# An attention layer with LayerNorm: four staging places for values, spread loads of x, other projection lists per gap, and loads issued by SyncE

## The chip, the core and the metric

The kernel runs on one core of a Trainium2 chip. The metric is the time of one execution on the device in microseconds (us).

## What is computed

One transformer layer for 16 images of 30 x 30 tokens of 512 features, 8 heads of 64, all in float32, with a bias on the scores that depends on the distance of two tokens on the grid:

```python
q, k, v = proj(wq, bq), proj(wk, bk), proj(wv, bv)     # x_seq @ w + b, split in 8 heads
scores = einsum('bhqd,bhkd->bhqk', q, k) / sqrt(d_k)
scores = scores + spatial_bias_matrix[None, None]      # by |dh| + |dw|
attn = softmax(scores, axis=-1)
ctx = einsum('bhqk,bhkd->bhqd', attn, v)
out = ctx @ wo + bo
resid = out + x_seq
out = (resid - mu) * rsqrt(var + 1e-5) * ln_gamma + ln_beta
```

## The kernel before

The images run one after the other through one software pipeline. Heads go in 4 pairs p. A pair's 30 rows of queries make 15 units, so an image has 60 units u, numbered 0 to 59. For one unit TensorE makes the scores of two heads against all 900 tokens (L684, 16 matmuls into one of two halves of s_ps), VectorE adds the bias and takes the least value (L966; q is negated), ScalarE takes the exponential and its sum (L803). The keys lie in two halves on different partitions, so their two maxima and sums are exchanged: SyncE issues four small DMAs own to other for two units together (L486, `exchange`), GpSimd finds the difference (L1099, L1102, `leads`), ScalarE its exponential (L811, `ratios`), GpSimd the weight (L1108 to L1113, `totals`), ScalarE scales the probabilities (L819, `normalise`), VectorE transposes them (L982, `turn`), and TensorE multiplies a group of up to five units by the values (L702, `context`), which ScalarE copies to ctx_sb (L831).

Every engine has a program of its own, written out in a fixed order by a function `body(im, u)`, called for u = 0 to 59 of each image. The engines stand in the same numbering but not at the same time, since they wait for each other by semaphores. In body u TensorE issues (u even only) the scores of units u+6 and u+7, then the contexts that `PV_UNITS` puts there, then the items that `GAPS[u]` lists; two bodies, u and u+1, are called a step here, by the even number. ScalarE does in body u: evictions that `EVICT` puts there, a context to keep, the exponentials of unit u+6, in odd bodies the ratios of u+3, the normalising of u+2, then issues of loads. VectorE: scores of u+6, the transpose of u, a turn of x, sums and norms of output tiles. GpSimd: totals or leads, 1/std, splits of x, bias, splits of the context. SyncE: stores of values, in odd bodies the exchange for u+5 (it waits for the exponentials of u+6), then stores, residual loads, loads of x.

The items of a gap are the projections, which share two banks of r_ps in turn in the order of `SEQUENCE`:
- ("piece", p, j), L603: half of k or half of q of pair p; pieces 4 and 5 belong to pairs 0 and 1 of the next image. ScalarE evicts it (L760, `keep_piece`). After the second half it issues the load of the next pair's weights, 512 KB (L741).
- ("value", t), L619: a tile of 120 or 90 tokens of v of the next image. ScalarE puts it into stage (L777, `stage_value`), which has two places, t % 2, and waits at L775 until the store of the tile two before has landed. SyncE stores it to v_dram (L478), from where ScalarE issues the loads of a pair's values by `LOADS`, four for a pair (L793).
- ("out", t), L645: an output tile of the image before. GpSimd splits the context into two float32r parts first (L1124, L1126, body by `SPLIT_UNITS`) and adds the bias to the residual (L1155), VectorE sums and normalises (L996 to L1010).

An item is evicted one body after its gap, a second item that is not an output tile two bodies after it. Float32 products are made of three float32r products, so an item has 12 matmuls.

x of the next image comes in 8 tiles of up to 128 tokens, four DMAs each (L496, `load_x`), into four places; VectorE turns it (L954, body `X_UNITS[t]` - 1) into x_turned, which lies in the last part of ctx_sb, and GpSimd splits it into xt (L1137, L1144, body `X_UNITS[t]`). Tiles 0 to 3 are loaded at `LOAD_X`, tiles 4 to 7 at `X_UNITS[t - 4]`, each as four issues in a row. Image 0 has no output tiles, the last one (image 15) no values and no pieces 4 and 5, and ends with its own output tiles ("final").

## Time and profile before

| | |
|---|---|
| median of 3 runs | 3177.74 us (3175.3 to 3180.98) |
| profiled execution, whole | 3174.42 us |
| its span | 3172.5 us |
| TensorE clock granted, mean | 0.991 of full |
| busy | TensorE 3027.3, VectorE 2649.1, ScalarE 2709.9, GpSimd 1615.2 us |
| DMA | 266.8 MB, mean 84 GB/s |

The span goes from the first instruction to the last end; the execution's own time has a little around it. Busy time is the sum of an engine's instructions; a wait lies in none of them, and "waiter <- releaser" in a row says which engine's result ended it. Matmuls overlap, and their ends are modelled. The windows view gives, for a stretch of time in us from the span's start, its length and then for TensorE's matmuls, its weight loads, VectorE, ScalarE and GpSimd the busy us and the instructions, then the granted clock (1.00 is full), the share of DMA engines busy and GB/s. "SPq" and "ACTq" are the queues in which SyncE and ScalarE issue DMAs; the us of such a line are the issuing, not the transfer.

### The profile page before, as it was taken

The numbers are of one execution on the slowest core, as the hardware profiler recorded it, in microseconds if no ns is written. First come the engines' busy times: TensorE is split into PE (matmuls) and PEld (weight loads), VectorE is DVE, ScalarE is ACT, GpSimd is POOL, SyncE is SP. The second block draws the span as 40 slices with busy tenths as digits, with TensorE's granted clock in tenths as the row PEclk, the third lists the DMA queues.
The fourth block names the chain that finished last, engine by engine and source line by source line (L and its number), as shares of the span: only waits on it lengthen the run. The fifth ranks groups of instructions, "written<-read, shape, count | busy, mean of one in ns | idle before, by whom it ended". The sixth has DMA issues, their size and how long they took to land.

```text
span 3172.5 us, 111090 instructions
## 1 busy us (share of the span) xinstructions
PE 3027.3 (95%) x44584; PEld 2073.6 (65%) x44584; DVE 2649.1 (84%) x5594; ACT 2709.9 (85%) x6839; POOL 1615.2 (51%) x3277
## 2 busy tenths in 40 slices
PE   7999999999999999999999999999999999999986
PEld 5666666666666666666666666666666666666654
DVE  3878889798897978879798897988979788797887
ACT  4988898888989888898888988888898898988885
POOL 1346445464553745546464454645536455464643
PEclk9999999999999999999999999999999999999998
DMA  7332423324243342323324233241433423233221
GB/s 206 72 82 73 99 63 95 81 71 109 57 97 85 78 98 68 86 78 92 88 73 102 60 95 84 76 104 54 97 82 78 102 69 90 74 91 89 73 66 28
DMA packets 523228, 266.81 MB, mean 84 GB/s; under 512 B 329274, under 2 KB 460346, under 8 KB 522590
## 3 DMA queue, kind: packets, MB, share of 16 engines
q1 hardware_dynamic: 375479, 127.82, 18.3%
q10 hardware_dynamic: 147232, 131.88, 14.1%
q8 instruction: 351, 5.75, 0.8%
q14 instruction: 166, 1.36, 0.1%
HBM read 194.10 MB, written 63.44 MB: 81 GB/s over the span
## 4 chain that ended last, share of the span: by engine, by line
PE 47%; DVE 15%; ACT 14%; SPq 11%; DMA 6%; issue 5%; POOL 2%; ACTq 0%; DVEq 0%
PE r_ps L603 13%; PE pv_ps L702 13%; PE s_ps L684 12%; ACT prob L803 7%; PE r_ps L645 6%; ACT prob L819 5%; SPq L496 5%; SPq L486 5%; DVE prob L966 5%; DVE prob_t L982 5%; DMA other<-own 4%; PE r_ps L619 3%; DVE stats L998 2%; DVE tokens L996 1%; DMA v_dram<-stage 1%
## 5 line engine op out<-in xcount | busy, mean ns | idle before, releaser
L803 ACT ACTIVATE prob<-prob,own 128x450 f32<-128x450 f32 x1920 | 1265.3, 662 | 142.3 <-DVE own L966 127.1
L966 DVE CUSTOM_DVE_ANT_0 prob<-s_ps,window 128x450 f32<-128x450 f32 x1920 | 1121.9, 621 | 286.1 <-PE s_ps L684 206.4
L982 DVE STREAM_TRANSPOSE prob_t<-prob 128x960 f32<-128x960 f32 x960 | 1126.6, 1174 | 140.1 <-ACT prob L819 139.8
L819 ACT ACTIVATE prob<-prob,weight 128x450 f32<-128x450 f32 x1920 | 1173.2, 660 | 52.8 <-POOL weight L1113 51.1
L684 PE MATMUL s_ps<-k_sb,q_sb 64*32 64x450 f32 x15360 | 856.4, 548 | 42.9 <-DVE own L966 39.9
L702 PEld LDWEIGHTS pv_ps<-prob_t,values 64*64 64x64 f32 x23040 | 730.0, 133 | 152.8 <-issue 80.1
L702 PE MATMUL pv_ps<-prob_t,values 64*64 64x150 f32 x23040 | 783.6, 290 | 8.5 <-DVE prob_t L982 8.4
L603 PE MATMUL r_ps<-xt,w_sb 128*128 128x450 f32 x3072 | 686.1, 373 | 27.5 <-ACT k_sb L760 13.5
L603 PEld LDWEIGHTS r_ps<-xt,w_sb 128*128 128x128 f32 x3072 | 572.1, 190 | 172.8 <-issue 69.8
L1099 POOL TENSOR_TENSOR lead<-own,other 128x4 f32<-128x4 f32 x480 | 96.6, 201 | 925.9 <-DMA other<-own 924.4
L1113 POOL TENSOR_TENSOR weight<-total,minus_one 128x4 f32<-128x4 f32 x480 | 501.0, 1044 | 37.6
L684 PEld LDWEIGHTS s_ps<-k_sb,q_sb 64*32 64x32 f32 x15360 | 229.0, 106 | 419.2 <-issue 296.1
L645 PE MATMUL r_ps<-wo_sb,ctx_split 128*120 128x512 f32 x1536 | 391.5, 405 | 32.1 <-DVE ctx_split L1017 10.9
L619 PE MATMUL r_ps<-wv_sb,xt 128*120 128x512 f32 (+1 forms) x1536 | 380.7, 400 | 18.2 <-POOL xt L1144 18.1
L645 PEld LDWEIGHTS r_ps<-wo_sb,ctx_split 128*120 128x120 f32 x1536 | 273.4, 184 | 175.5 <-issue 84.4
L619 PEld LDWEIGHTS r_ps<-wv_sb,xt 128*120 128x120 f32 (+1 forms) x1536 | 262.2, 176 | 158.9 <-issue 64.8
L803 ACT ACTIVATION_READ_ACCUMULATOR prob<-prob,own 128x1 f32 x1920 | 364.0, 190 | 0.0
L1108 POOL TENSOR_TENSOR total<-ratio,other 128x4 f32<-128x4 f32 x480 | 111.8, 233 | 424.7 <-ACT ratio L811 406.9
L811 ACT ACTIVATE ratio<-lead 128x4 f32<-128x4 f32 x480 | 94.1, 196 | 95.5 <-POOL lead L1102 94.0
L1155 POOL TENSOR_TENSOR tokens<-tokens,bo_all 120x512 f32<-120x512 f32 x120 | 160.6, 1344 | 0.0
L966 DVE DVE_READ_ACCUMULATOR2_ANT own<- 128x1 f32 x1920 | 157.6, 82 | 0.0
L1126 POOL TENSOR_TENSOR ctx_split<-ctx_sb,ctx_split 128x480 fp32r<-128x480 f32 x120 | 145.0, 1209 | 9.8
(63 smaller groups left out, 1475.9 us busy)
## 6 DMA issues: line engine op xcount, KB each, us to landing
w_sb<-w_split ACTq DMA_DIRECT2D x126, 512.0 KB, 3.9
values<-v_dram ACTq DMA_DIRECT2D x256, 240.0 KB, 3.3
other<-own SPq DMA_DIRECT2D x1920, 1.0 KB
tokens<-in_x SPq DMA_DIRECT2D x420, 64.0 KB, 2.6
tokens<-in_x SPq DMA_DIRECT2D x109, 240.0 KB, 3.6
out<-tokens SPq DMA_DIRECT2D x105, 240.0 KB, 2.8
v_dram<-stage SPq DMA_DIRECT2D x90, 240.0 KB, 3.0
v_dram<-stage SPq DMA_DIRECT2D x30, 180.0 KB, 2.3
```

The lines of the kernel that those rows point to most:

```text
L486: sp.dma_start(other[QUAD * a:QUAD * a + QUAD, s, :, :], own[QUAD * c:QUAD * c + QUAD, s, :, :]).then_inc(exchanged[s], 16)
L603: last = pe.matmul(r_ps[:, bank, 0:HALF], w_sb[:, kind, a, k, :], xt[:, c, k, columns(half)], start=(k == 0 and i == 0), stop=(k == KT - 1 ...
L619: last = pe.matmul(r_ps[0:n, bank, :], xt[:, a, k, at:at + n], wv_sb[:, c, k, :], start=(k == 0 and i == 0), stop=(k == KT - 1 and i == PA ...
L645: last = pe.matmul(r_ps[0:TT, bank, :], ctx_split[:, t % 2, a, k, :], wo_sb[:, c, k, :], start=(k == 0 and i == 0), stop=(k == PAIRS - 1 a ...
L684: last = pe.matmul(s_ps[row:row + QUAD, u % 2, head, 0:HALF], q_sb[d, p % 2, q0:q0 + QUAD], k_sb[d, p % 2, columns(r)], start=True, stop=T ...
L702: last = pe.matmul(pv_ps[d, a, 0:n * GRID].rearrange("d (u w) -> d u w", u=n), values[half, p % 2, j, d], prob_t[half, g % 2, 0:n, head, Q ...
L803: nc.scalar.activation(prob[:, im.unit(u) % RING, head, 0:HALF], prob[:, im.unit(u) % RING, head, 0:HALF], ACT.Exp, scale=-1.0, bias=own[: ...
L819: nc.scalar.activation(prob[:, im.unit(u) % RING, head, 0:HALF], prob[:, im.unit(u) % RING, head, 0:HALF], ACT.Copy, scale=weight[:, s, c: ...
L966: nc.vector.tensor_tensor_reduce(prob[:, im.unit(u) % RING, head, 0:HALF], s_ps[:, u % 2, head, 0:HALF], window[:, w0:w0 + HALF // GRID, : ...
L982: nc.vector.transpose(out=prob_t[:, g % 2, v % PER_GROUP, :, :].rearrange("p h k -> p (h k)"), in_=prob[:, im.unit(u) % RING, :, :].rearra ...
L1113: nc.gpsimd.tensor_tensor(weight[:, s, :], total[:, s, :], minus_one[:, :], ALU.pow).then_inc(weight_done, 1)
L1155: nc.gpsimd.tensor_tensor(y, y, bo_all[0:rows(t), :], ALU.add).then_inc(res_bias, 1)
```

## The change

- Values go through four staging places, `STAGE_SLOT`, the third and fourth in the part of ctx_sb where x_turned lay. x_turned now lies where ctx_split does. The waits are changed to fit.
- `LOAD_X` has eight entries; a tile's four DMAs are issued two in that body, two in the next. `X_UNITS` is later from tile 3 on.
- `GAPS` has another list of items for each gap, with `SPLIT_UNITS` to fit. Output tiles come in pairs at 14 and 22, pieces in pairs at 18, 24, 28, 48 and 54, values in pairs at 32, 38 and 42.
- The loads of weights and values inside the images are issued by SyncE, behind the exchange of the same body, and not by ScalarE. A residual is loaded six bodies after an output tile's eviction and not five.

```diff
-SPLIT_UNITS = [0, 0, 3, 5, 6, 10, 13, 15]
-LOAD_X = [20, 22, 26, 29]
-X_UNITS = [30, 31, 32, 33, 34, 36, 38, 40]
+SPLIT_UNITS = [0, 0, 3, 5, 9, 13, 15, 16]
+LOAD_X = [24, 26, 29, 31, 33, 35, 37, 39]
+X_UNITS = [30, 31, 32, 36, 37, 40, 41, 43]
+STAGE_SLOT = [0, 1, 2, 3, 0, 1, 0, 1]
+STAGES = 4
...
-GAPS = {2: pieces(1, (3,)) + [out(0)], 4: [out(1), out(2)], 8: [out(3)] + pieces(2, (0,)), 12: [out(4)] + pieces(2, (1,)),
-        14: [out(5)] + pieces(2, (2,)), 18: [out(6)] + pieces(2, (3,)), 22: [out(7)] + pieces(3, (0,)),
-        24: pieces(3, (1, 2)), 28: pieces(3, (3,)), 32: [value(0), value(1)], 34: [value(2), value(3)],
-        38: [value(4), value(5)], 42: [value(6)] + pieces(4, (0,)), 44: pieces(4, (1, 2)), 48: pieces(4, (3,)),
-        52: [value(7)] + pieces(5, (0,)), 54: pieces(5, (1,)), 58: pieces(5, (2,))}
+GAPS = {2: [out(0)] + pieces(1, (3,)), 4: [out(1)], 8: [out(2)] + pieces(2, (0,)), 12: [out(3)] + pieces(2, (2,)),
+        14: [out(4), out(5)], 18: pieces(2, (3, 1)), 22: [out(6), out(7)], 24: pieces(3, (0, 2)), 28: pieces(3, (3, 1)),
+        32: [value(0), value(1)], 34: [value(2)], 38: [value(3), value(4)], 42: [value(5), value(6)], 44: pieces(4, (2,)),
+        48: pieces(4, (0, 1)), 52: pieces(4, (3,)) + [value(7)], 54: pieces(5, (0, 1)), 58: pieces(5, (2,))}
...
             def load_values(im, p, n):
...
+                if n == 0:
+                    if p == 0:
+                        for i in range(STAGES):
+                            sp.wait_ge(v_kept[i], kept_in(i, b + 1))
+                    if pair > 1:
+                        sp.wait_ge(pv_full, PAIR_GROUPS * (pair - 1))
...
+                for work in im.evicted(u):
+                    if work[0] == "piece" and PIECES[work[2]][1] and not (im.last and work[1] == PAIRS - 1):
+                        next_weights(im, *work[1:])
...
+                if u in LOADS and not (im.last and LOADS[u][0] == PAIRS):
+                    load_values(im, *LOADS[u])
                 for work in im.out_tiles(u - 4) + im.finals(u - 2):
                     store(im, work)
-                for work in im.out_tiles(u - 5):
+                for work in im.out_tiles(u - 6):
...
+                    for t in range(X_TILES):
+                        if u == LOAD_X[t] and t >= SLOTS:
+                            sp.wait_ge(x_turn, X_TILES * im.b + t - SLOTS + 1)
...
+                        for a in range(128 // QUAD):
+                            if u == LOAD_X[t] + a // 2:
+                                load_x(im.b + 1, t, a)
...
-                    act.wait_ge(v_kept[t % 2], 16 * (NT // 2 * (im.b + 1) + t // 2))
+                    i = STAGE_SLOT[t]
+                    if i >= 2 and im.first:
+                        act.wait_ge(wq_kept, 16 * 2 * PAIRS)
+                    elif i >= 2:
+                        act.wait_ge(split_lo, NT * im.b)
+                    act.wait_ge(v_kept[i], kept_in(i, im.b + 1) + 16 * STAGE_SLOT[:t].count(i))
...
                 if g == GROUPS - PAIR_GROUPS - 1 and not im.last:
-                    act.wait_ge(x_lo, X_TILES * (im.b + 1))
+                    for i in range(2, STAGES):
+                        act.wait_ge(v_kept[i], kept_in(i, im.b + 2))
...
-                elif t == 0:
-                    dve.wait_ge(split_lo, NT * im.b)
+                if t == 0 and not im.first:
+                    use = ("out", NT - 1)
+                    dve.wait_ge(bank_full[bank_of(use)], im.use(use) + 1)
```

## Rows read from the trace of the kernel before

**Rows 1.** The page: busy time by engine, shares of the chain by engine.

```profile
PE 3027.3 (95%) x44584; PEld 2073.6 (65%) x44584; DVE 2649.1 (84%) x5594; ACT 2709.9 (85%) x6839; POOL 1615.2 (51%) x3277
...
PE 47%; DVE 15%; ACT 14%; SPq 11%; DMA 6%; issue 5%; POOL 2%; ACTq 0%; DVEq 0%
```

**Rows 2.** Windows view, images 1 to 14: busy us by engine (instructions), clock, DMA, GB/s.

```profile
254.47:2955.66 2701.19, 2621.35 (x38977) 1797.94 (x38976) 2302.51 (x4876) 2358.08 (x5972) 1434.30 (x2889) 1.00 0.33 83
```

**Rows 3.** Windows view, image 7: steps 4, 8, 34, 44; then 10, 14, 24, 28, 38.

```profile
1426.31:1435.01 8.70, 7.73 (x57) 4.69 (x56) 8.28 (x17) 7.12 (x18) 8.05 (x15) 1.00 0.21 63
1440.67:1448.81 8.14, 7.32 (x60) 4.75 (x56) 7.85 (x18) 7.26 (x21) 5.68 (x10) 1.00 0.21 54
1524.59:1532.64 8.05, 7.64 (x58) 4.39 (x57) 5.86 (x12) 5.55 (x14) 5.13 (x9) 1.00 0.45 71
1559.13:1567.60 8.47, 7.11 (x58) 4.84 (x57) 5.14 (x11) 8.17 (x20) 2.29 (x7) 1.00 0.27 74
1448.81:1454.47 5.66, 5.66 (x154) 4.27 (x153) 5.41 (x11) 4.32 (x13) 4.24 (x7) 1.00 0.50 140
1461.93:1469.03 7.10, 7.10 (x57) 4.84 (x56) 6.85 (x16) 5.14 (x13) 6.61 (x13) 1.00 0.39 111
1494.72:1501.48 6.76, 6.76 (x57) 4.92 (x56) 6.55 (x14) 6.10 (x16) 2.54 (x8) 1.00 0.64 141
1507.14:1511.48 4.34, 4.34 (x48) 2.66 (x44) 3.23 (x9) 4.20 (x13) 1.43 (x4) 1.00 0.31 73
1538.29:1545.73 7.44, 7.44 (x60) 4.76 (x56) 3.87 (x8) 4.91 (x14) 2.13 (x4) 1.00 0.58 169
```

**Rows 4.** Waits of TensorE in images 1 to 14: us, times, longest.

```profile
PE s_ps L684 <- DVE own L966: 20.5, 25, 1.5
PE r_ps L619 <- POOL xt L1144: 15.1, 13, 2.1
PE r_ps L645 <- POOL ctx_split L1126: 9.7, 14, 1.0
PE r_ps L645 <- ACT q_sb L760: 9.3, 12, 1.7
PE pv_ps L702 <- DVE prob_t L982: 8.4, 17, 0.8
PE r_ps L603 <- ACT k_sb L760: 7.6, 13, 0.8
PE r_ps L603 <- ACT stage L777: 6.9, 14, 0.5
```

**Rows 5.** Waits of ScalarE in images 1 to 14.

```profile
ACT prob L803 <- DVE own L966: 108.4, 101, 3.5
ACT ratio L811 <- POOL lead L1102: 76.4, 81, 3.1
ACT stage L777 <- DMA v_dram<-stage: 65.7, 28, 3.5
ACT prob L819 <- POOL weight L1113: 46.8, 57, 2.1
```

**Rows 6.** Timeline of SyncE's queue, image 7: start, us, engine, line, operation, count.

```profile
1517.20 6.10 SPq L496 DMA_DIRECT2D tokens<-in_x  x8
1523.34 2.53 SPq L486 DMA_DIRECT2D other<-own  x4
```

**Rows 7.** Timeline of GpSimd after the exchange issued at 1523.34.

```profile
1527.10 0.20 POOL L1099 TENSOR_TENSOR lead<-own,other 128x4 f32<-128x4 f32 x1 [2.75 <-DMA other<-own]
```

**Rows 8.** Timelines of SyncE, ScalarE, GpSimd, image 7: an exchange beside a weight load.

```profile
1461.95 3.64 SPq L486 DMA_DIRECT2D other<-own  x4
...
1462.28 0.34 ACTq L741 DMA_DIRECT2D w_sb<-w_split  x1
...
1467.88 0.20 POOL L1099 TENSOR_TENSOR lead<-own,other 128x4 f32<-128x4 f32 x1
```

**Rows 9.** The page: a weight load, KB, median us from issue to landing.

```profile
w_sb<-w_split ACTq DMA_DIRECT2D x126, 512.0 KB, 3.9
```

More of the change, by code:

```diff
@@ L171, in groups @@
         before = [] if self.first else [(Before(self), g) for g in pv_groups(u + UNITS)]
-        return before + [(self, g) for g in pv_groups(u, self.last) if u < UNITS or self.last]
+        return before + [(self, g) for g in pv_groups(u) if u < UNITS or self.last]
     def background(self, u):
@@ L279, in attention_layernorm @@
         ctx_sb = sb("ctx_sb", [128, PAIRS, S])
+        with nc.sbuf_tensor("x_turned", [128, 2, D], F32) as x_turned:
+            pass
         ctx_split = sb("ctx_split", [128, 2, 2, PAIRS, TT], F32R)
@@ L383, in attention_layernorm @@
         v_staged = sem("v_staged")
-        v_kept = [sem(f"v_kept{i}") for i in range(2)]
+        v_kept = [sem(f"v_kept{i}") for i in range(STAGES)]
         v_in = [sem(f"v_in{i}") for i in range(2)]
@@ L418, in staged, with kept_in @@
             n = value_rows(t)[2]
-            return turned_flat[0:n, t * D:t * D + D] if im is pro else stage[0:n, t % 2, :]
+            return turned_flat[0:n, t * D:t * D + D] if im is pro else (
+                stage[0:n, STAGE_SLOT[t], :] if STAGE_SLOT[t] < 2 else stage_too[0:n, STAGE_SLOT[t] - 2, :])
+        def kept_in(i, images):
+            return 16 * STAGE_SLOT.count(i) * images
         def out_no(im, work):
@@ L477, in keep_value @@
                         sp.wait_ge(v_in[i], 64 * PAIRS // 2 * im.b)
-                sp.dma_start(v_dram[(im.b + 1) % 2, half, j:j + n, :], staged(im, t)).then_inc(v_kept[t % 2], 16)
+                sp.dma_start(v_dram[(im.b + 1) % 2, half, j:j + n, :], staged(im, t)).then_inc(v_kept[STAGE_SLOT[t]], 16)
             def exchange(im, x):
@@ L593, in piece @@
                     first_xt_ready(NT - 1)
-                if j == 0 and p == PAIRS and im is not pro:
-                    pe.wait_ge(x_lo, X_TILES * (im.b + 1))
+                if p == PAIRS and im is not pro:
+                    pe.wait_ge(x_lo, X_TILES * im.b + x_tiles_to(HALF * (half + 1)))
                 if half == 0:
@@ L672, in scores @@
                         if mine:
-                            pe.wait_ge(bank_free[bank], mine[-1])
+                            pe.wait_ge(bank_free[bank], max(mine))
                         elif p == 1:
@@ L761, in keep_piece @@
                                      bias=bias[:, p % PAIRS:p % PAIRS + 1]).then_inc(bank_free[bank], 1)
-                if half and not (im is pro and p == PAIRS) and not (im.last and p == PAIRS - 1):
+                if half and im is pro and p > PAIRS:
                     next_weights(kind, p)
@@ L779, in stage_value @@
                 act.nop(nofuse=True).then_inc(v_staged, 1)
-            def load_values(im, p, i):
-                b, p = (im.b, p) if p < PAIRS else (im.b + 1, 0)
-                pair = PAIRS * b + p
-                if i == 0:
-                    if p == 0:
-                        for bank in range(2):
-                            act.wait_ge(v_kept[bank], 16 * NT // 2 * (b + 1))
-                    if pair > 1:
-                        act.wait_ge(pv_full, PAIR_GROUPS * (pair - 1))
-                a, r = divmod(i, 2)
-                row = 2 * QUAD * a + QUAD * r
-                act.dma_start(values[row:row + QUAD, p % 2, :, :],
-                              v_dram[b % 2, r, :, 128 * p:128 * p + 128].rearrange("(j k) d -> k j d", k=QUAD)
-                              ).then_inc(v_in[p % 2], 16)
             def exponentials(im, u):
@@ L901, in body @@
                     return
-                if im.first and u == 0:
-                    use = ("bv_wo", 0)
-                    act.wait_ge(bank_full[bank_of(use)], pro.use(use) + 1)
-                    act.wait_ge(lo_done["wo"], 1)
-                    for i in range(4):
-                        load_values(im, 0, i)
-                if u in LOADS and not (im.last and LOADS[u][0] == PAIRS):
-                    load_values(im, *LOADS[u])
                 for t in range(NT):
@@ L977, in turn @@
                 if im.first and u == 0:
-                    for i in range(2):
-                        dve.wait_ge(v_kept[i], 16 * NT // 2)
+                    for i in range(STAGES):
+                        dve.wait_ge(v_kept[i], kept_in(i, 1))
                 if v % PER_GROUP == 0 and not known(group, 1):
@@ L1132, in x_split_hi @@
                 if t == 0:
-                    for use in pieces(PAIRS - 1, (2, 3)):
+                    for use in pieces(PAIRS - 1):
                         pool.wait_ge(bank_full[bank_of(use)], im.use(use) + 1)
@@ L1182, in body @@
                         x_split_lo(im, t)
-                for work in im.out_tiles(u + 2):
+                for work in (im.out_tiles(1) if u == 0 else []) + im.out_tiles(u + 2):
                     add_bias(im, work)
```

57 lines of the change are left out of this document (35 added, 22 removed).

## The prediction

> **What bounds the kernel now.** I read the page first. TensorE is busy 3027.3 us, 95% of the span, VectorE and ScalarE 84% and 85%, and the chain that ended last runs through TensorE for only 47% and touches every engine, SyncE's queue with 11% [rows 1]. So TensorE paces the kernel, and the others touch it at places; the question is which places, and what each costs. For that the windows view over images 1 to 14, which run the same program: 2701.19 us, 192.94 an image, TensorE busy 2621.35, 187.2 an image, clock 1.00 throughout [rows 2]. ScalarE is busy 2358.1 / 14 = 168.4 us an image and VectorE 164.5.
>
> Then single steps. A step is two units: TensorE issues two units of scores and after them a context group, or one or two of what a gap lists (piece, value or output tile). Without a stall a step takes 5.66 us with a context, 4.34 with one piece, 6.76 with two, 7.10 with a piece and an output tile, 7.44 with two value tiles; in all five TensorE's busy time is the whole window [rows 3]. An output or value tile alone makes 7.10 - (6.76 - 4.34) = 4.68. The old lists have 12 context steps, 8 mixed ones, 2 with two pieces, 4 with one piece and 4 with two tiles: 12 x 5.66 + 8 x 7.10 + 2 x 6.76 + 4 x 4.34 + 4 x 7.44 = 185.4 us. An image takes 192.9, so stalls cost 7.6 us an image. TensorE's named waits sum to 77.9 us in 14 images, 5.6 an image [rows 4]; the other 2.0 are matmuls stretched beside a wait. In image 7 step 4 is 8.70 instead of 7.44, step 8 8.14 instead of 7.10, step 34 8.05 instead of 7.44, step 44 8.47 instead of 6.76 [rows 3].
>
> **The change part by part.**
>
> *New list of projections.* Its work is the same, only grouped otherwise: 12 context steps, 5 with two tiles, 5 with two pieces, 4 mixed, 2 with one tile, 2 with one piece: 67.9 + 37.2 + 33.8 + 28.4 + 9.4 + 8.7 = 185.4 us. Nothing is gained on TensorE itself, all of it is in the stalls.
> - Step 4 held out(1) and out(2). Out(2)'s split is GpSimd's, in body 3, and came late 14 times of 14, 9.7 us; the first waited for ScalarE to empty its bank, 9.3 us [rows 4]. Now step 4 holds out(1) alone, and out(2) comes at step 8, four bodies later. Both waits go: 1.3 us by image 7.
> - Step 8's stall is the second set of scores waiting for VectorE (20.5 us at 25 places, most of them here). VectorE has two output tiles to sum and one to normalise around step 6 and is busy 7.85 of step 8's 8.14 us [rows 3]. The new list has such doubles at 14 and 22. Behind 22 stands a step of 6.76 instead of 5.66, so VectorE has 1.1 us more, which is what the stall costs here: nothing there. Behind 14 stands a context step as before, but out(3) is now first in its step and not second, so VectorE gets it a piece (2.4 us) earlier. Between 0 and the 1.04 us of step 8; I take 0.4, nearer to nothing, since the 2.4 us are more than the stall.
> - Step 44 had two pieces straight behind a value and a piece; each bank was emptied by ScalarE just too late (7.6 + 6.9 us), and ScalarE is busy 8.17 of 8.47 us there [rows 3, 4]: it was behind. Now 44 has one piece, 42 two values, 48 two pieces with a context step between. Gone, 1.7 us by image 7. New pairs in neighbouring steps are 12/14, 22/24, 52/54. In the first two the later pair's first item wants the bank of an item that VectorE empties, as at the old 12 and 14, where step 14 took its bare 7.10; at 52/54 a piece has only the value tile (2.8 us) behind it before the next image's first scores want it. If ScalarE is late by more there, step 54 stalls; old step 54 is preceded by a full step of slack. 0 to 1.1 us; I take 0, since ScalarE has longer steps (6.76, 7.10) to catch up in.
>
> *Four staging places.* ScalarE waited for the store of two tiles earlier 28 times, 65.7 us, 2.35 each [rows 5], and it is in order: exponentials, normalising and evictions queue behind it, and VectorE's transposes and TensorE's contexts (8.4 us, steps 40 and 0) behind these. With four places, and value tiles spread over 32 to 42, a place is filled again four bodies after it was filled or later, where it is two now; a body is 3.2 us and the wait 2.35, so one body more would do. The wait goes. TensorE gets back its own part, the context waits, 0.6 an image; in image 0, which has no output tiles, ScalarE paces, and there the 2 x 2.35 = 4.7 us count fully. Places 2 and 3 lie where the turned x lay; the waits put in for that (split_lo, v_kept before a context is kept) are for things done several bodies earlier. Cost 0.
>
> *Spread loads of x.* An exchange of row statistics costs SyncE 2.53 us for its four issues; eight loads of x in a row cost 6.10, so 0.76 each [rows 6]. Of the 32 of an image 20 stand in bodies 29 to 33, and exchanges queued behind: the wait of ScalarE's ratio for lead is 76.4 us in 81 places [rows 5]. The lateness went on to GpSimd's splits of x and from there to value tiles at 32 and 34, 15.1 us [rows 4]. Now each body from 24 to 40 has at most two loads: per step 2.53 + 4 x 0.76 = 5.6 us. The tightest stretch is steps 34 to 38, 4.68 + 5.66 + 7.44 = 17.8 us: there SyncE has 3 x 5.6 and seven single issues (value stores and loads, a residual), at 0.34 to 0.76 each 2.4 to 5.3, together 19 to 22. SyncE is late there by 1 to 4 us, against over 6 behind the eight loads of rows 6. Price: x of tile 2 arrives nearly when VectorE turns it (issued in body 30, turned in 31), up to 2 us of VectorE with nothing queued that TensorE needs before step 34; no cost. For value tiles whose x is split in the same step (31/32, 37/38, 41/42) between 0 and the 1.1 us an image they cost today; I take 0.3.
>
> *Loads issued by SyncE.* ScalarE's issue of 0.34 us ran beside its activations (0.34 us at 1462.28) [rows 8], so taking 24 away gives ScalarE 0 to 24 x 0.34 = 8.2 us; I take 0, because the queue's issue isn't in its busy time. SyncE gets the 8.2 us; it holds 30 x 2.53 = 76, x loads of 32 x 0.76 = 24 and some 24 other issues of 0.34 to 0.76, 8 to 18 (an estimate), so it goes from 56 to 61% of an image to 60 to 66%. What is queued behind an issue is the next exchange. In SyncE's order all of these loads stand behind an exchange, none just ahead of one. That helps: clean, lead starts 1.23 us after the exchange's last issue (1525.87 to 1527.10) [rows 6, 7]; with a weight load issued by ScalarE into its middle, it is 1465.59 to 1467.88, 2.3 us, and the four issues took 3.64 us instead of 2.53 [rows 8]. I count no gain of its own for that: it pays for the risk. SyncE's new waits (a piece's bank full, v_kept, pv_full) are all for events before the exchange that it has just waited for.
>
> The Trainium skill speaks against this part. "DMA: Bandwidth & Descriptors", section "Queues, rings and completion order", says that SP and ACT each have one ring on the same 16 engines, that a ring is consumed in order, and that an engine takes turns between rings. So a small exchange behind a weight load of its own ring would have to wait for all of it, where today it takes turns. [...] It is the second rival below.
>
> **The sum,** against the profiled execution (3172.5 us span, 3174.4 in all, 3.3 below the median of 3177.7). Stalls that stay: 0.4 + 0.3 + 0.2 (contexts at 0 and 40) = 0.9 of 7.6 us, so 6.7 us an image, 94 in 14. Image 15 has steps 4 and 8: 2.3. Image 0: 4.7. Together 101: 3073.4, on the median's scale 3077.
>
> **Rivals.**
> 1. *The stalls move.* The doubles at 14 and 22 each make a stall of step 8's size (1.04), the three second value tiles one of step 34's (0.61), the new neighbour at 54 one of 1.1: 2.1 + 1.8 + 1.1 = 5.0 against 7.6, a gain of 2.6 x 14 + 7 = 43: 3134. For it: the pattern exists today; against it: each has more slack than its old twin. Half of it is as likely as all: 3105 to 3134.
> 2. *The exchange becomes the bound (slower).* If the loads keep the next exchange's packets waiting, each of 16 value loads by 1.1 us and each of 8 weight loads by 2.2 (2.3 - 1.2 seen once, doubled for the whole ring), ScalarE waits 35 us more for ratio an image. Its own total today is 168.4 + (76.4 + 46.8) / 14 = 177.2, so it would need 212 with nothing hidden, and with half hidden 195; against 192.9 that is +2 x 14, 3205. It decides from 0.65 us for each of the 24 loads, since ScalarE has 15.7 us to spare. Against it: between the end of one exchange and the next start there are about 3.9 us (a mean step of 6.4 less 2.5), and a weight load lands in 3.9 [rows 9].
> 3. *It does not do what it says:* SyncE, blocked on the exchange, issues loads so late that they are waited for, or the four places only shift ScalarE's wait to VectorE (108.4 us of ScalarE's waits are for VectorE already [rows 5]). Then within some us of today: 3178.
>
> **How the numbers follow.** Forecast 3077 with its own range 3060 (no stall stays) to 3100 (2.5 us an image stay): 0.65. Rival 1: 0.21. Rival 3: 0.04. Rival 2: 0.10. Range 3058 to 3134, which leaves out rivals 2 and 3 and the ends of the others. Faster by over 0.2% (about what a measurement of this kernel can tell from no change): 0.86; within: 0.03; slower: 0.11.
>
> **What would show it.** After the change: an image of 186 to 187.5 us with TensorE's waits under 1.5; no wait of stage for v_dram; ratio's wait for lead at most half; the waits of L645 for ctx_split and for q_sb gone, as that of pieces for k_sb; scores waiting for VectorE at step 18 under 0.4 us. Wrong: ratio waits of over 2 us behind SyncE's loads, VectorE's double at 14 showing over 1 us at step 18, or second value tiles waiting for x. The prediction fails high if step lengths without stall grow over 5.66, 6.76 and 7.44.

## The result, and the profile after

| | before | after |
|---|---|---|
| median | 3179.4 us (3175.3 to 3185.0, 4 runs) | 3256.2 us (3245.6 to 3259.9, 4 runs) |
| ratio, 95% interval | | 1.0239 (1.022 to 1.0259) |
| profiled execution, span | 3172.5 us | 3258.1 us |
| an image, mean of 14 | 192.94 us | 199.12 us |
| granted TensorE clock, mean | 0.991 | 0.978 |

The change costs 77 us, where 101 were to be gained. The two spans differ by 85.6 us: 14 x 6.18 = 86.5 in images 1 to 14, 2.4 more ahead of image 0, 2.4 less in it and 0.9 less in the last image and the end.

First the page of after: busy time, shares of the chain, groups of instructions, DMA issues (count, KB, median us from issue to landing).

```profile
PE 3060.8 (94%) x44584; PEld 2085.6 (64%) x44584; DVE 2643.7 (81%) x5594; ACT 2707.4 (83%) x6839; POOL 1599.1 (49%) x3277
...
PE 41%; SPq 14%; ACT 13%; DVE 12%; DMA 8%; issue 6%; POOL 6%; DVEq 0%; ACTq 0%; POOLq 0%
...
w_sb<-w_split SPq DMA_DIRECT2D x123, 512.0 KB, 4.7
...
tokens<-in_x SPq DMA_DIRECT2D x420, 64.0 KB, 3.2
```

TensorE has the same 44584 matmuls and is busy 33.5 us longer [rows 1]; SyncE's queue and DMA have grown in the chain, from 11 and 6% to 14 and 8%. A weight load lands 4.7 us after its issue instead of 3.9 [rows 9].

The windows view of after: images 1 to 14; then steps 4, 8, 18, 32 and 34 of image 7, a part of step 34, and steps 42 and 44.

```profile
254.47:3042.16 2787.69, 2656.68 (x38977) 1812.38 (x38976) 2296.81 (x4873) 2354.51 (x5966) 1418.92 (x2884) 0.98 0.32 81
1462.46:1467.13 4.67, 4.67 (x46) 2.59 (x45) 4.43 (x13) 4.64 (x13) 4.02 (x6) 1.00 0.02 1
1473.69:1482.52 8.83, 7.31 (x57) 4.75 (x57) 8.54 (x18) 8.83 (x26) 5.13 (x12) 1.00 0.16 44
1508.63:1516.41 7.78, 7.03 (x60) 4.79 (x57) 7.49 (x18) 7.26 (x20) 3.52 (x8) 1.00 0.15 36
1554.38:1566.04 11.66, 7.74 (x60) 4.63 (x57) 4.71 (x12) 4.77 (x13) 5.44 (x10) 1.00 0.62 133
1566.04:1574.81 8.77, 7.35 (x44) 3.74 (x45) 8.34 (x17) 8.11 (x21) 3.15 (x8) 0.61 0.22 45
1567.06:1573.88 6.82, 5.43 (x25) 3.09 (x26) 6.39 (x16) 6.58 (x17) 1.84 (x6) 0.50 0.15 38
1593.52:1605.03 11.51, 9.24 (x60) 5.74 (x56) 7.56 (x17) 8.10 (x21) 4.71 (x13) 0.85 0.38 106
1605.03:1609.35 4.32, 4.32 (x46) 2.67 (x46) 3.08 (x8) 3.74 (x9) 1.38 (x3) 1.00 0.32 82
```

Steps 4 and 44 are bare, as forecast. Step 8 takes 8.83 us where 8.14 were and 7.10 expected; step 18, behind the pair of output tiles, 7.78 for a bare 6.76. The large losses are at 32 (11.66 for 7.44), 34 (8.77 for 4.68) and 42 (11.51 for 7.44). In step 32 VectorE and ScalarE are busy less than half of the time: they wait too.

The waits of after in images 1 to 14, first of TensorE, then of the others (us in total, times, longest).

```profile
PE s_ps L727 <- DVE own L990: 120.3, 89, 3.4
PE r_ps L688 <- POOL ctx_split L1150: 6.8, 11, 1.2
PE r_ps L662 <- POOL xt L1168: 3.2, 6, 0.8
...
DVE x_turned L978 <- DMA tokens<-in_x: 184.9, 65, 7.3
...
ACT prob L835 <- DVE own L990: 189.4, 112, 7.2
ACT prob L851 <- POOL weight L1137: 139.4, 79, 6.2
ACT ratio L843 <- POOL lead L1126: 35.2, 51, 1.7
...
POOL tokens L1179 <- DMA tokens<-in_x: 78.4, 28, 5.3
```

TensorE waits for little but VectorE's treatment of scores, six times as long as before (20.5 us [rows 4]), and VectorE's own long wait is for x: 184.9 us at its turn, L978. An image has 13.2 us of it: 2.6 at the turn of tile 1, 6.4 at tile 2, 2.8 at tile 6, 1.4 at the others. The stall can be followed in image 7. SyncE's queue and VectorE (start, us, engine, line, operation, in brackets the idle time before it and who ended it):

```profile
1555.47 0.59 SPq L503 DMA_DIRECT2D w_sb<-w_split  x1
1556.10 1.61 SPq L528 DMA_DIRECT2D tokens<-in_x  x2
1557.77 0.61 SPq L503 DMA_DIRECT2D w_sb<-w_split  x1
1558.43 1.26 SPq L528 DMA_DIRECT2D tokens<-in_x  x2
...
1555.48 0.71 DVE L978 STREAM_TRANSPOSE x_turned<-tokens 128x512 f32<-128x512 f32 x1 [3.40 <-DMA tokens<-in_x]
1557.18 1.17 DVE L1006 STREAM_TRANSPOSE prob_t<-prob 128x960 f32<-128x960 f32 x1
1564.20 0.71 DVE L978 STREAM_TRANSPOSE x_turned<-tokens 128x512 f32<-128x512 f32 x1 [5.85 <-DMA tokens<-in_x]
```

and TensorE beside them:

```profile
1557.32 0.99 PE L727 MATMUL s_ps<-k_sb,q_sb 64*32 64x450 f32 x16 [1.96 <-DVE own L990]
1558.24 5.84 PE L662 MATMUL r_ps<-wv_sb,xt 128*120 128x512 f32 x24
1566.04 0.99 PE L727 MATMUL s_ps<-k_sb,q_sb 64*32 64x450 f32 x16 [1.96 <-DVE own L990]
1568.45 1.75 PE L727 MATMUL s_ps<-k_sb,q_sb 64*32 64x450 f32 x16 [1.42 <-DVE own L990]
1570.14 4.74 PE L662 MATMUL r_ps<-wv_sb,xt 128*120 128x512 f32 x12
```

The four loads of x's tile 2 go in two pairs, each right behind a 512 KB weight load. The last is issued by 1559.69 and the tile is there at 1564.20, 4.5 us later. VectorE has been ready since 1558.35. Behind the turn stand, in VectorE's order, the biased scores of units 38 and 39, and TensorE can't write units 40 and 41 over them before: it has two value tiles to do, finishes them at 1564.08 and stands still to 1566.04 and again before 1568.45. The last of TensorE's lines shows what follows: a value tile of 12 matmuls at 4.74 us, where a pair of them took 5.84 just before.

The first stall in step 32, 1.96 us before 1557.32, has another source: the turn of tile 1 at 1555.48, which waited 3.40 us. No weight load is near that tile, whose second half is issued at 1551.13; it is issued late and turned soon. On the mean of 14 images TensorE stands still 1.2 us before the scores of unit 39, behind tile 1, and 2.4 and 1.2 us before those of 40 and 41, behind tile 2.

Over the 14 images I set the start of each even unit's scores against the bare step lengths of [rows 3]. That gives the loss per image by groups of steps, for this kernel and all others but x_early, residual_early and tail_residual_6:

| us per image, steps | 0, 2 | 4 | 6, 8 | 12-18 | 20-30 | 32, 34 | 36-42 | 44 | sum |
|---|---|---|---|---|---|---|---|---|---|
| before | 0.6 | 1.6 | 1.3 | 0.5 | 0 | 1.4 | 0.7 | 1.4 | 7.6 |
| after | 0 | 0 | 2.3 | 1.4 | 0 | 7.6 | 2.5 | 0 | 13.8 |
| loads_scalar | 0 | 0 | 2.3 | 2.3 | 0 | 0.9 | 2.6 | 0 | 8.1 |
| before_loads_sync | 0 | 1.6 | 1.5 | 0.7 | 0 | 1.7 | 0.6 | 1.4 | 7.6 |
| before_staging | 0.6 | 1.9 | 1.2 | 0.5 | 0 | 1.3 | 0.1 | 1.0 | 6.6 |
| weights_scalar | 0 | 0 | 2.2 | 1.5 | 0.1 | 2.5 | 2.9 | 0 | 9.2 |
| loads_last | 0 | 0 | 2.2 | 1.8 | 0 | 3.0 | 3.9 | 0 | 10.8 |
| turn_later | 0 | 0 | 2.3 | 1.5 | 0 | 4.7 | 2.0 | 0 | 10.5 |
| two_weights_later | 0 | 0 | 2.1 | 1.5 | 0.1 | 1.7 | 8.5 | 0 | 13.8 |
| two_weights_at_31 | 0 | 0 | 2.1 | 1.5 | 0 | 1.6 | 4.0 | 0 | 9.2 |
| lists_mended | 0 | 0 | 2.5 | 1.9 | 0.1 | 0 | 1.2 | 0 | 5.7 |
| mended_unpaired | 0 | 0 | 2.4 | 0.2 | 3.1 | 0.1 | 1.7 | 0 | 7.5 |
| staging_spread | 0.1 | 1.5 | 1.5 | 0.6 | 0 | 2.8 | 0.2 | 0 | 6.8 |
| staging_tail | 0 | 1.4 | 1.7 | 0.4 | 0 | 1.2 | 0 | 0 | 4.8 |

(Steps 46 to 58 are within 0.1 everywhere.) From before to after 0.6 + 1.6 + 1.4 = 3.6 us an image are gained at 0 to 4 and at 44, and 6.2 + 1.8 + 1.0 + 0.9 = 9.9 lost at 32 and 34, 36 to 42, 6 and 8, and 12 to 18: 6.3, against 6.2 by the period.

### The profile page after: what moved, and what is told of

Read it like the earlier page. It is cut to its first block, busy times and chain, and to the rows that moved or that the text cites. A ratio compares the mean times of both kernels' runs of the same rounds, so it can differ in the third digit from the quotient of the medians.

```text
span 3258.1 us, 111151 instructions
## 1 busy us (share of the span) xinstructions
PE 3060.8 (94%) x44584; PEld 2085.6 (64%) x44584; DVE 2643.7 (81%) x5594; ACT 2707.4 (83%) x6839; POOL 1599.1 (49%) x3277
## 4 chain that ended last, share of the span: by engine, by line
PE 41%; SPq 14%; ACT 13%; DVE 12%; DMA 8%; issue 6%; POOL 6%; DVEq 0%; ACTq 0%; POOLq 0%
PE r_ps L646 11%; PE s_ps L727 11%; PE pv_ps L745 10%; SPq L494 7%; ACT prob L835 7%; DMA tokens<-in_x 6%; PE r_ps L662 6%; ACT prob L851 5%; DVE prob L990 5%; DVE prob_t L1006 4%; SPq L528 4%; PE r_ps L688 3%; DMA other<-own 2%; POOL tokens L1179 1%; POOL weight L1137 1%
## 5 line engine op out<-in xcount | busy, mean ns | idle before, releaser
L727 PE MATMUL s_ps<-k_sb,q_sb 64*32 64x450 f32 x15360 | 876.6, 555 | 150.6 <-DVE own L990 149.4
L646 PE MATMUL r_ps<-xt,w_sb 128*128 128x450 f32 x3072 | 674.3, 373 | 5.7 <-ACT prob_t L825 3.7
L662 PE MATMUL r_ps<-wv_sb,xt 128*120 128x512 f32 (+1 forms) x1536 | 401.5, 417 | 3.5 <-POOL xt L1168 3.5
L662 PEld LDWEIGHTS r_ps<-wv_sb,xt 128*120 128x120 f32 (+1 forms) x1536 | 280.3, 187 | 150.4 <-issue 65.5
L978 DVE STREAM_TRANSPOSE x_turned<-tokens 128x512 f32<-128x512 f32 x120 | 77.6, 647 | 199.2 <-DMA tokens<-in_x 198.8
```

The source lines that it names most:

```text
L646: last = pe.matmul(r_ps[:, bank, 0:HALF], w_sb[:, kind, a, k, :], xt[:, c, k, columns(half)], start=(k == 0 and i == 0), stop=(k == KT - 1 ...
L662: last = pe.matmul(r_ps[0:n, bank, :], xt[:, a, k, at:at + n], wv_sb[:, c, k, :], start=(k == 0 and i == 0), stop=(k == KT - 1 and i == PA ...
L727: last = pe.matmul(s_ps[row:row + QUAD, u % 2, head, 0:HALF], q_sb[d, p % 2, q0:q0 + QUAD], k_sb[d, p % 2, columns(r)], start=True, stop=T ...
```

## The experiments

Ratios are to the kernel before on the same chip, with 95% intervals. In the cuts of code below `...` stands for what is left out, also inside a line, and what stands behind `#` is my note.

| | median us | ratio |
|---|---|---|
| loads_scalar | 3183.4 | 1.0015 (1.000 to 1.003) |
| before_loads_sync | 3175.4 | 0.9993 (0.9981 to 1.0005) |
| x_early | 3231.2 | 1.0168 (1.0149 to 1.0186) |
| before_staging | 3155.2 | 0.9932 (0.9918 to 0.9947) |
| two_weights_later | 3268.0 | 1.0288 (1.0268 to 1.0307) |
| residual_early | 3248.8 | 1.0224 (1.0198 to 1.0249) |
| lists_mended | 3146.3 | 0.9897 (0.9874 to 0.992) |
| staging_tail | 3134.2 | 0.9864 (0.9847 to 0.988) |
| weights_scalar | 3198.1 | 1.0055 (1.0031 to 1.0079) |
| loads_last | 3219.9 | 1.0132 (1.010 to 1.0164) |
| turn_later | 3213.3 | 1.0101 (1.0078 to 1.0124) |
| staging_spread | 3161.0 | 0.9935 (0.9911 to 0.9959) |
| two_weights_at_31 | 3200.0 | 1.007 (1.0053 to 1.0087) |
| mended_unpaired | 3173.6 | 0.9984 (0.9975 to 0.9994) |
| tail_residual_6 | 3136.5 | 0.9869 (0.9854 to 0.9884) |

**Which part costs it.** Two small parts of the change, one value load issued in body 56 and not 55 and pieces 4 and 5 waiting for no more of x than they read, are in every kernel made from after, and no run takes them apart. loads_scalar is after with the weight and value loads issued by ScalarE again:

```diff
-                for work in im.evicted(u):
-                    if work[0] == "piece" and ...:
-                        next_weights(im, *work[1:])          # sp
...
+                if half and not (im is pro and p == PAIRS) and not (im.last and p == PAIRS - 1):
+                    next_weights(kind, p)                    # act; load_values too
```

> The changed kernel, but weights and values are loaded by ScalarE again, in the bodies in which they were. Theory A (x is loaded too few bodies before VectorE turns it; VectorE waits for it 184.9 us in 14 images of the changed kernel and TensorE's scores behind it): the loads of x keep their places, so most of the wait stays, 100 us or more, and the time is 3200 to 3250. Theory B (weights, values, x and exchanges in one queue of SyncE: two weight loads are issued just ahead of the second half of x tile 2): VectorE's wait for x falls under 50 us and the time to 3180 or below.

3183.4 us: 73 of the 77 us are gone (1.0239 to 1.0015), so theory A is not the whole of it. VectorE's wait for x fell from 184.9 to 94.8 us, not under 50. before_loads_sync does the opposite, that part alone on the kernel before (SyncE's `next_weights` and `load_values` as in the change):

> The kernel before, with only the issue of weights and values moved to SyncE. Theory B: most of the loss is here, 3230 to 3260. Theory A: x tiles 0 to 3 are loaded early as before, so within 15 us of the kernel before, 3165 to 3195.

3175.4, no difference that can be measured, so theory B alone isn't it either. The loads on SyncE cost nothing by themselves, and the rest of the change costs 5.7 us by itself (3183.4 - 3177.7); the 73 us are of the two together. In before_loads_sync x is issued as early as ever. In before tile 2 of x had been issued 9.9 us ahead of step 32's start on the mean of 14 images, VectorE was ready to turn it at 1.3 and waited 0.2. In after the last issue is at 4.9, 15 us later, VectorE is ready at 3.2 and waits 6.4. loads_scalar has the same lists and late issues: last issue at 1.1, a wait of 1.3.

**Is it the lateness of x?** x_early issues the first tiles earlier, all else as after:

```diff
-LOAD_X = [24, 26, 29, 31, 33, 35, 37, 39]
+LOAD_X = [20, 22, 28, 30, 33, 35, 37, 39]
```

> The changed kernel with LOAD_X = [20, 22, 28, 30, 33, 35, 37, 39] instead of [24, 26, 29, 31, ...]: x tiles 0 to 3 one to four bodies earlier, all loads still by SyncE. Theory A: VectorE's wait for x in step 32 (116 us of 185) goes down by 80 or more, steps 32 and 34 lose 5 of their 7.7 us of excess, and the time is 3150 to 3190. Theory B: the queue only moves its lateness, the time stays over 3220.

3231.2: a third of the loss gone. Theory A had 3150 to 3190, theory B over 3220. It isn't the clean test I meant. SyncE stood still for the place of tiles 2 and 3, since output tiles 6 and 7 are now made at 22 and stored only in body 27 (waits of SyncE in x_early):

```profile
SPq L494 <- ACT prob L835: 925.8, 385, 7.6
SPq L528 <- DMA out<-tokens: 67.2, 28, 4.1
```

So tile 2's last issue came at 4.3 and not ahead of the turn. The new list of projections holds x back too; LOAD_X alone can't undo it. turn_later moves the other end, the turn of tile 2, one body back:

```diff
-X_UNITS = [30, 31, 32, 36, 37, 40, 41, 43]
+X_UNITS = [30, 31, 33, 36, 37, 40, 41, 43]
```

> The changed kernel with x tile 2 turned and split one body later (X_UNITS[2] = 33 instead of 32), loads where they were. If VectorE's in-order wait for tile 2 is what stops the scores in steps 32 and 34 (7.7 us an image), one body (3.2 us) more takes off 3 us an image of VectorE's wait and 30 to 60 us of the time: 3195 to 3225. If the value tile of step 34 then waits for the split instead, nothing is won: 3240 to 3260.

3213.3: the wait falls from 6.4 to 4.1 us and the loss at 32 and 34 from 7.6 to 4.7 an image. What stands behind the waiting turn counts, and how long it waits.

**Number or place of the loads.** weights_scalar gives only the eight weight loads of an image back to ScalarE, the 16 value loads stay:

```diff
-                if half and im is pro and p > PAIRS:
+                if half and not (im is pro and p == PAIRS) and not (im.last and p == PAIRS - 1):
                     next_weights(kind, p)
```

> The changed kernel with only the weight loads (8 an image, 512 KB) issued by ScalarE again; values stay with SyncE. The measured 73 us between all loads by SyncE (3256) and by ScalarE (3183) come from weight loads ahead of x tile 2 and of the last residual in SyncE's one ring: then this recovers 50 or more of the 73, under 3205. If it is the number of issues on SyncE (16 value loads are 2 of 3), it recovers about a third, 3225 to 3240.

3198.1: 58 of the 77 us gone. Tile 2 waits 1.0 us, its data there 1.9 us after the last issue, not 4.6. That looks as if a queue of their own kept the weights out of x's way, but the trace shows another reason. ScalarE issues the two weight loads of bodies 29 and 30 earlier than SyncE did, 7.9 and 3.0 us ahead of step 32's start on the mean, where SyncE issued them 0.9 and 3.0 us behind it. They now fall beside tile 1, and although they stand in the other queue that tile lands late: 4.7 us after its last issue on the mean, in after 2.7, with the same value load and stores of output ahead of it in SyncE's queue. Image 5 of weights_scalar, queues of SyncE and ScalarE, then VectorE:

```profile
1128.15 2.39 SPq L528 DMA_DIRECT2D tokens<-in_x  x2
1126.23 0.33 ACTq L781 DMA_DIRECT2D w_sb<-w_split  x1
1128.69 0.33 ACTq L781 DMA_DIRECT2D w_sb<-w_split  x1
1136.68 0.71 DVE L975 STREAM_TRANSPOSE x_turned<-tokens 128x512 f32<-128x512 f32 x1 [4.80 <-DMA tokens<-in_x]
```

The last part of tile 1 is issued by 1130.54 and there only 6.1 us later. It took 5.4 to 6.8 us in the five images in which the second weight load was issued less than 2 us ahead of that point, 2.7 to 4.7 in the other nine. The 2.5 us an image that are still lost at step 32 are tile 1's. loads_last leaves all on SyncE, but puts them behind everything else of a body:

```diff
+                for work in im.evicted(u):     # moved from ahead of store(im, work)
+                    if work[0] == "piece" and ...: next_weights(im, *work[1:])
+                if u in LOADS and ...: load_values(im, *LOADS[u])
```

> The changed kernel with the same issues on SyncE, but weights and values come last in a body, behind stores, residuals and x. Ring order theory: the second weight load of step 30 no longer stands ahead of the second half of x tile 2, nor the one of body 20 ahead of anything late; VectorE's wait for tile 2 (6.4 us an image) falls by 2 to 4 and the time to 3200 to 3230. Number-of-issues theory: nothing changes, 3245 to 3260.

3219.9, nearly half of the loss gone, as expected of the order within SyncE's queue; but steps 36 to 42 lose 3.9 us an image instead of 2.5. The issues of tile 2 end at 2.9 instead of 4.9, but it is turned at 6.7 all the same, 3.9 us after the last issue: the weight load of body 29 now stands behind the tile's first half and still just ahead of its second. Then only the two weight loads that meet tile 2, of bodies 29 and 30, were moved, seven bodies back in one kernel and two in the other:

```diff
+                late = {36: (PAIRS - 1, 3), 37: (PAIRS - 1, 1)}     # two_weights_later
+                late = {31: (PAIRS - 1, 3), 32: (PAIRS - 1, 1)}     # two_weights_at_31
                 for work in im.evicted(u):
+                    if ... and work[1:] not in late.values():
+                if u in late and not im.last:
+                    next_weights(im, *late[u])
```

> The changed kernel, all loads by SyncE, but the two weight loads of bodies 29 and 30 (of 24 loads an image) are issued in bodies 36 and 37. If those two, standing among the halves of x tile 2 in one ring, are what makes tile 2 late, VectorE's wait for it (6.4 us an image) falls under 3, steps 32 and 34 lose 3 to 5 of 7.7 us of excess: 3190 to 3215. If it is the sum of the issues on SyncE, 3240 to 3260.

3268.0, no gain at all, and outside both expectations. The table shows why: the loss at 32 and 34 fell from 7.6 to 1.7, and that of 36 to 42 rose from 2.5 to 8.5. The loads now stood next to tile 6, whose wait rose from 2.8 to 5.3 us. Steps 32 and 42 of image 7 in two_weights_later:

```profile
1551.65:1561.03 9.38, 7.67 (x60) 4.64 (x56) 6.54 (x15) 6.54 (x17) 6.60 (x12) 1.00 0.26 40
...
1585.99:1600.29 14.30, 9.23 (x60) 5.27 (x56) 7.56 (x17) 9.06 (x23) 5.10 (x14) 0.88 0.63 135
```

> As two_weights_later, but the two weight loads of pair 3's last pieces are issued in bodies 31 and 32, ahead of the halves of x tile 3, which waits 9 us in its place until VectorE turns it. Ring theory (it is what stands ahead of a tile that is turned one or two bodies later): neither tile 2 nor tile 6 is delayed, steps 32 to 42 lose 5 to 7 us of their 10 of excess, 3165 to 3195. Sum-of-issues theory: 3240 to 3270, as for two_weights_later (3268).

3200.0, 5 us above the expected range: 56 of the 77 us gone, by moving two loads out of 24, ahead of tile 3, which is turned four bodies after tile 2 and has time. Tile 2 waits 2.4, tile 6 2.3; tile 2 is there 1.8 us after its last issue. With all loads on SyncE this comes to the same 9.2 us lost an image as weights_scalar. So it isn't that SyncE issues the large loads that costs the time, but how close they are issued to a tile that VectorE waits for. That their place in the one queue matters beside the moment of issue is not shown: every edit here that moved the one moved the other.

**The residuals.** GpSimd's 78.4 us of waiting for residuals are new. A residual is issued a body later and between two weight loads (SyncE's queue and GpSimd in after, image 7):

```profile
1520.58 0.59 SPq L503 DMA_DIRECT2D w_sb<-w_split  x1
1521.21 0.88 SPq L539 DMA_DIRECT2D out<-tokens  x2
1522.14 0.42 SPq L532 DMA_DIRECT2D tokens<-in_x  x1
1522.61 1.22 SPq L503 DMA_DIRECT2D w_sb<-w_split  x1
...
1528.81 1.28 POOL L1179 TENSOR_TENSOR tokens<-tokens,bo_all 60x512 f32<-60x512 f32 x1 [5.29 <-DMA tokens<-in_x]
```

residual_early loads it at u - 5 again:

```diff
-                for work in im.out_tiles(u - 6):
+                for work in im.out_tiles(u - 5):
```

> The changed kernel with a residual loaded five bodies after the eviction and not six. GpSimd waits 78 us in 14 images for the residuals of output tiles 5 and 7 (none of that before the change). If ScalarE's lateness from there (its wait for weight is 139 us instead of 47) delays SyncE's exchange and x behind it, 15 to 40 us come back: 3215 to 3240. If it is absorbed before step 30, 3245 to 3260.

3248.8: GpSimd's wait for residuals, 78.4 us, is gone (no such wait is left in images 1 to 14), and the time went down by 7, within the two intervals. Nearly all of that wait was idle time of an engine that nobody waited for.

**The parts without the collision.** before_staging is before with nothing but the four places (`STAGE_SLOT`, `stage_too`, the waits on v_kept):

> The kernel before, with only the four staging places (x turned beside ctx_split, its waits with it). By the prediction ScalarE's wait for the store (65.7 us in 14 images) goes; TensorE gets back 0.6 us an image and image 0 gets 4.7: 3160 to 3170. If the wait only moves to VectorE or GpSimd: 3175 to 3185.

3155.2, 22 us less, 5 below the expected range. ScalarE's wait for the store is gone, image 0 takes 175.5 us instead of 180.7, and 1.0 us an image are gained. staging_spread adds the loads of x in halves, at bodies where they are in time, with the old lists:

```diff
-LOAD_X = [20, 22, 26, 29]
+LOAD_X = [20, 22, 25, 28, 30, 32, 34, 36]
...
+                            if u == LOAD_X[t] + a // 2:
+                                load_x(im.b + 1, t, a)
```

> The kernel before with four staging places (3155) and the loads of x spread in halves, LOAD_X = [20, 22, 25, 28, 30, 32, 34, 36], X_UNITS and lists of before. If the burst of 20 issues in bodies 29 to 33 is what makes exchanges late (6.6 us) and the value tiles of steps 32 and 34 wait (1.4 us an image of excess), 3130 to 3145. If tile 3 and 4 now arrive late instead, 3150 to 3175.

3161.0, nothing on top of the places: the stalls at 34 and 44 went and one at 32 came, since tiles 3 and 4 in halves were now waited for by 2.4 and 2.3 us (0.7 and 0.4 in before_staging). staging_tail keeps tiles 0 to 4 whole and splits only 5 to 7, and turns tiles 6 and 7 a body later:

```diff
-LOAD_X = [20, 22, 26, 29]
-X_UNITS = [30, 31, 32, 33, 34, 36, 38, 40]
+LOAD_X = [20, 22, 26, 29, 30, 32, 34, 37]
+WHOLE = 5
+X_UNITS = [30, 31, 32, 33, 34, 36, 39, 41]
...
+                            if u == LOAD_X[t] + (a // 2 if t >= WHOLE else 0):
+                                load_x(im.b + 1, t, a)
```

> The kernel before with four staging places; x tiles 0 to 4 loaded whole and early (the fifth in body 30), only tiles 5 to 7 spread: LOAD_X = [20, 22, 26, 29, 30, 32, 34, 37], X_UNITS 39 and 41 for the last two. If the spread in halves lost its gain at step 32 through tile 4 (2.9 us an image of excess) and its gains at 34 and 44 stay (2 us), 3125 to 3145, the fastest of all. If exchanges are late behind the eight issues of 29 and 30 as before, 3150 to 3160.

3134.2, the fastest: 41 us less than before in the same runs, and 122 less than after. Images 1 to 14 of it:

```profile
250.33:2911.90 2661.57, 2612.42 (x38977) 1799.98 (x38976) 2294.28 (x4873) 2354.65 (x5965) 1429.51 (x2885) 1.00 0.34 85
```

190.11 us an image, TensorE busy 186.6 of them. tail_residual_6 is this with residuals at u - 6, so that SyncE blocks less on stores:

> staging_tail (3134) with residuals loaded six bodies after the eviction, so that SyncE no longer blocks on the store that it has just issued (105 us of its waits in the kernel before). If that blocking delays exchanges, 3122 to 3130. If it is hidden in SyncE's idle time, 3130 to 3138.

3136.5, the same. SyncE's waiting there is hidden.

**What the new list is worth.** lists_mended has the new list and places, the loads on ScalarE, x early enough, the stores of output tiles at u - 3 so that they don't hold x back, and residuals at u - 5:

```diff
-LOAD_X = [24, 26, 29, 31, 33, 35, 37, 39]
+LOAD_X = [20, 22, 28, 30, 32, 34, 36, 38]
...
-                for work in im.out_tiles(u - 4) + im.finals(u - 2):
+                for work in im.out_tiles(u - 3) + im.finals(u - 2):
```

> The changed lists and staging with weights and values on ScalarE (3183), x loads one to four bodies earlier (LOAD_X = [20, 22, 28, 30, 32, 34, 36, 38]), output tiles stored three bodies after eviction and residuals loaded after five. If late x is the rest of what the new lists lose (2.3 + 0.9 us of excess in steps 38 and 32), 3140 to 3160. If the new lists lose at steps 8 and 18 by themselves (VectorE's output tiles, 1.8 + 1.9 us), not under 3150 in any case; and no better than the old lists with staging (3155).

3146.3: 9 us less than before_staging, with x spread as well, and 12 more than staging_tail, which has the old list. Steps 4, 32, 34 and 44 are bare here, but 6 and 8 lose 2.5 us an image and 12 to 18 1.9. mended_unpaired takes the pair of output tiles at 14 apart:

```diff
-        14: [out(4), out(5)], 18: pieces(2, (3, 1)),
+        14: [out(4)] + pieces(2, (3,)), 18: [out(5)] + pieces(2, (1,)),
```

> lists_mended (3146) with output tiles 4 and 5 no longer both at 14: 14 holds out(4) and a piece, 18 holds out(5) and a piece. If step 18's 1.8 us an image are VectorE's two output tiles at 14, they go: 25 us, 3115 to 3128. If it is VectorE's whole load, the stall moves to a later step and the time stays over 3138.

3173.6, worse as a whole, though steps 12 to 18 lose 0.2 instead of 1.9: the pair was the cause of that stall. (The kernel also loads tile 1 of x at 24 and not at 22, behind those steps.) Output tile 5 four bodies later opened another. GpSimd's split of tile 7 is in body 16 and overwrites what tile 5 reads, so it waited for tile 5's matmuls, and lead and weight waited behind it (GpSimd in mended_unpaired, image 7):

```profile
1461.14 0.87 POOL L1201 TENSOR_TENSOR rstd<-var_eps,constants 120x1 f32<-120x1 f32 x1
1469.92 0.38 POOL L1161 CAST ctx_split<-ctx_sb 128x240 fp32r<-128x240 f32 x1 [7.91 <-PE r_ps L677]
1470.38 0.70 POOL L1163 TENSOR_TENSOR ctx_split<-ctx_sb,ctx_split 128x240 fp32r<-128x240 f32 x1
1471.04 0.20 POOL L1136 TENSOR_TENSOR lead<-own,other 128x4 f32<-128x4 f32 x1
```

Steps 20 to 30 lose 3.1 us an image by it. Both move one wait and make another. A version with the split of tile 7 moved as well was not run.

## Why the prediction was wrong

- **"x of tile 2 arrives nearly when VectorE turns it ..., up to 2 us of VectorE with nothing queued that TensorE needs before step 34; no cost."** This step failed, and it is most of the error: steps 32 and 34 lose 7.6 us an image, 106 of the 179 us between 3077 and 3256. The wait was 6.4 us on the mean, and VectorE is in order: behind the turn stand biased scores, and TensorE's next scores at 34 need the banks of the first of them. I priced a late arrival at its own length, on one engine, without asking where it stands in that engine's order. Two things made it longer. SyncE was late: the last issue came 4.9 us into step 32, where before it came 9.9 us ahead of it. And the data came 4.6 us after that issue, where it is 1.8 with no weight load near (two_weights_at_31). For tile 1, issued in bodies 26 and 27 and turned in 30, the prediction had no term at all; its wait of 2.6 us is behind the first stall in step 32, 1.2 us on the mean.
- **"What is queued behind an issue is the next exchange."** That was the wrong list. In SyncE's queue the loads of x and the residuals of the same body stand behind a weight load as well. The second rival was near the mechanism, a small load delayed by a large one, and had the wrong victim: the exchange has a whole step of time. ScalarE's wait of ratio for lead fell to 35.2 us, though the rival would have it grow by 35 an image.
  The Trainium skill's rule, weighed in the prediction ("DMA: Bandwidth & Descriptors", section "Queues, rings and completion order": a ring is consumed in order, an engine takes turns between rings), was read there to mean that a small load waits for a large one of its own ring and takes turns with one of the other. The runs don't bear out that difference. Behind weight loads of its own queue tile 2 took 4.6 us after its last issue, and 3.9 where only one of the two stood ahead of a part of it (loads_last); but with them in ScalarE's queue at about the same moment tile 1 took 4.7 (weights_scalar) and 4.2 (loads_scalar). How the engines divide their time between the two rings no run here shows.
- **The parts were priced one by one.** By themselves the loads on SyncE cost -2 us and the rest +6; together 77. Two edits that both use up the slack of one transfer (one issues it late, the other puts a weight load just ahead of it) don't add. The sum had no term for that.
- **Steps 4 and 8, "Both waits go: 1.3 us", and step 8's stall taken to move to 14 and 22.** Half right. The waits of step 4 went, and 1.6 us an image with them. But step 6 and 8 lose 2.3 us, not 0. I reckoned that out(2) coming later gives VectorE room; what I left out is that step 4 became 4.0 us shorter (8.70 to 4.67), time in which VectorE had worked off its queue. It has two units a step, some 4.8 us (in step 4 of image 7 it starts one unit at 1463.56 and the next at 1465.97), whatever TensorE does, more than the 4.67 that step 4 now lasts. In step 8 it is busy 8.54 of 8.83 us: there it is the bound. That the stall at 4 had paid for it is my reading; in the table all kernels with the new list lose nothing at 4 and 2.1 to 2.5 at 6 and 8, all with the old one 1.4 to 1.9 and 1.2 to 1.7, but no run tests it by itself.
- **Step 18, "0.4".** A term that was too small: 1.4 us an image in after at 12 to 18 (2.3 in loads_scalar), as the first rival had it; mended_unpaired showed that the pair at 14 is the cause. Behind the pair at 22 there was nothing, as forecast. With these two the new list gained nothing in the steps with output tiles, 4 to 18: 3.4 us in before, 3.7 in after.
- **The clock** was not in the sum. TensorE's busy time in 14 images rose by 35.3 us (2621.35 to 2656.68) at the same number of matmuls, so of 86.5 us more 51.2 are waiting and 35.3 matmuls that took longer. In image 7 the granted clock is 1.00 up to the stall at the end of step 32, then 0.61 on the mean of step 34: for the 6.8 us from 1567.06 it is at the lower of the two levels, 1.2 instead of 2.4 GHz. In step 42 it is again 0.85, and TensorE is busy 9.24 us for a bare 7.44. By the trace's clock records TensorE was at the lower level for 96 of the 2788 us of these images, in before for 7 of 2701. The prediction took bare step lengths for granted after a stall.
- **Second value tiles, "0.3".** The size is right, 3.2 us in 14 images are TensorE's wait for xt, but what the term meant to cover is small beside VectorE's wait for the same x.
- **Right:** the stalls at 0, 40 and 44 are gone; the wait for the store is gone, and by itself worth 22 us where its terms give 4.7 + 14 x 0.6 = 13 (image 0: 5.2; the others 1.0 each); ratio's wait is under half. The third rival named loads issued too late, but at a time like today's.
- **Small slips in the working.** The range's lower end, "3060 (no stall stays)", should have been 3064 by its own terms (3177.7 less 14 x 7.6 and 7). And of SyncE's new waits, taken to be "all for events before the exchange", one cost 7.7 us in 13 places: L518, a value load, for the contexts.

What stays open: how much of the clock's loss would go if the stall were half as long. two_weights_at_31, with 4.6 us less lost an image, has TensorE busy 2629.4 and a clock of 1.00 on the mean, but still 0.85 in step 32 of image 7; that is no measure of the relation.

## What to carry to other kernels

When a DMA is moved to another queue, work out when it will be issued there and list everything that is issued near it, in either queue, not only what is most urgent, and for each the time between its last issue and its consumer; a bulk load must not be issued close to a transfer whose slack another edit has used up. Price a late arrival by what is queued behind the waiting instruction on its in-order engine, and try such edits alone and together. When a stall is removed, ask which engine had used it to catch up: it will ask for that time a step later.

## What the runs showed of the hardware

- A tile of x (four issues, 256 KB) was there 1.8 us after its last issue with no weight load near (tile 2 of two_weights_at_31), and 4.6 us with a 512 KB weight load just ahead of each half in the same queue (tile 2 of after). The other queue was no shelter: tile 1 took 4.7 us on the mean with the weight loads issued by ScalarE at about that moment (weights_scalar), 2.7 where none was near (after). A weight load itself takes 4.7 us by the page of after, 3.9 by that of before.
- In image 7 a stall of 1.96 us on TensorE was followed by 0.99 us of matmuls and then by the granted clock at half for 6.8 us, the next stall of 1.42 us in it: a value tile of 12 matmuls took 4.74 us, where two had just taken 5.84. I had not reckoned with a stall costing its matmuls as well.
- A weight load issued by SyncE costs its queue 0.59 to 0.61 us in these lines, where ScalarE's issue took 0.34 [rows 8]. The prediction had taken 0.34 to 0.76 for it.
